# Attention on TensorE: the last four transposes of a unit moved between the two halves of the next scores

## The reference, cut to what matters

```
q, k, v = (x @ Wq + bq), (x @ Wk + bk), (x @ Wv + bv)      # 16 heads of 32
scores = einsum('bhqd,bhkd->bhqk', q / sqrt(32), k) + attention_bias   # (2, 16, 2048, 2048)
scores = where(mask, -inf, scores)
probs = softmax(scores, axis=-1)
ctx = einsum('bhqk,bhkd->bhqd', probs, v)
```

## Time and profile before

| what | value |
|---|---|
| median of 3 runs | 3473.58 us (3472.29 to 3478.68) |
| the profiled execution | 3475.8 us, span 3474.0 us |
| TensorE matmuls busy | 3408.8 us, 98% |
| GpSimd busy | 2395.8 us, 69% |
| VectorE busy | 2343.6 us, 67% |
| ScalarE busy | 2278.9 us, 66% |
| TensorE, transposes of probabilities (L1288) | 8192, 1023.6 us |
| TensorE, scores (L1267) | 2048, 700.7 us |
| TensorE, V products (L1307) | 16384, 500.3 us |

### The profile page before, as it was taken

How to read it: one execution, slowest core, us unless ns; L and a number is a source line. 1 busy time by engine, 2 the same in 40 slices (tenths; PEclk the granted TensorE clock), 3 DMA queues, 4 the chain that set the end, 5 groups by cost and what they waited for, 6 DMA issues and landing times. The chain is left out here.

```text
span 3474.0 us, 84659 instructions
## 1 busy us (share of the span) xinstructions
PE 3408.8 (98%) x33299; PEld 2692.7 (78%) x33299; DVE 2343.6 (67%) x5039; ACT 2278.9 (66%) x3399; POOL 2395.8 (69%) x942
## 2 busy tenths in 40 slices
PE   7999989999999999999999999999999999999998
PEld 3444448888888888888888888888778888887886
DVE  7776758888888888888888888888623232332333
ACT  2433449999999999999999999999622212221321
POOL 1222249999999999999999999999643324232322
PEclk8999999999999999999999999999999999999998
DMA  6666599888898988898888998888644544564463
GB/s 215 225 235 239 197 367 349 325 337 331 333 401 329 338 331 333 341 389 337 332 332 329 367 370 334 331 327 329 246 144 154 167 137 157 164 191 143 154 210 124
DMA packets 342721, 954.80 MB, mean 275 GB/s; under 512 B 33204, under 2 KB 190004, under 8 KB 267576
## 3 DMA queue, kind: packets, MB, share of 16 engines
q1 hardware_dynamic: 337108, 940.95, 73.4%
q10 hardware_dynamic: 5220, 8.42, 0.6%
HBM read 849.63 MB, written 99.62 MB: 273 GB/s over the span
## 5 line engine op out<-in xcount | busy, mean ns | idle before, releaser
L1249 POOL TENSOR_TENSOR at_tiles<-at_tiles,at_negmask 128x1920 f32<-128x1920 f32 x509 | 1950.7, 3896 | 29.9 <-DMA at_tiles<-in_bias 19.0
L1349 ACT ACTIVATE at_tiles<-at_tiles,at_rmin 128x2048 f32<-128x2048 f32 x512 | 1030.5, 2013 | 2.4 <-DVE at_rmin L1409 2.4
L1288 PE MATMUL at_ps_p<-consts,at_tiles 128*128 128x128 f32 x8192 | 1023.6, 272 | 1.7 <-ACT at_prob_t L1359 1.3
L1288 PEld LDWEIGHTS at_ps_p<-consts,at_tiles 128*128 128x128 f32 x8192 | 936.3, 139 | 72.5 <-DVE at_prob_t L1420 2.0
L1359 ACT ACTIVATE at_prob_t<-at_ps_p 128x512 f32<-128x512 f32 x1664 | 898.2, 603 | 125.0 <-PE at_ps_p L1288 124.9
L1409 DVE CUSTOM_DVE_ANT_0 at_tiles<-at_ps_s,at_tiles,at_rmin 128x1024 f32<-128x1024 f32 x512 | 655.0, 1279 | 171.7 <-PE at_ps_s L1273 171.0
L1267 PE MATMUL at_ps_s<-at_k_stack,at_q_stack 128*128 128x512 f32 x2048 | 700.7, 438 | 8.1 <-DVE at_rmin L1409 6.1
L1409 DVE CUSTOM_DVE_ANT_0 at_tiles<-at_ps_s,at_tiles 128x1024 f32<-128x1024 f32 x512 | 623.9, 1219 | 24.5 <-POOL at_tiles L1249 22.2
L1307 PE MATMUL at_ps_c<-at_prob_t,at_v 128*32 128x128 f32 x16384 | 500.3, 274 | 1.0 <-DVE at_ctx_rows L1437 1.0
L1307 PEld LDWEIGHTS at_ps_c<-at_prob_t,at_v 128*32 128x32 f32 x16384 | 431.6, 110 | 44.2 <-issue 43.0
L1267 PEld LDWEIGHTS at_ps_s<-at_k_stack,at_q_stack 128*128 128x128 f32 x2048 | 310.8, 191 | 62.5 <-issue 51.5
(11 more groups left out here) (239 smaller groups left out, 4098.3 us busy)
## 6 DMA issues: line engine op xcount, KB each, us to landing
at_tiles<-in_bias SPq DMA_DIRECT2D x512, 1024.0 KB, 6.3
ff_w_card<-w_mix SPq DMA_DIRECT2D x256, 256.0 KB, 2.7
ff_w_card<-in_W SPq DMA_DIRECT2D x192, 256.0 KB, 2.9
at_k_stack<-k_hi SPq DMA_DIRECT2D x128, 256.0 KB, 5.6
at_k_stack<-k_lo SPq DMA_DIRECT2D x128, 256.0 KB, 5.6
negm<-em_mask_out SPq DMA_DIRECT2D x32, 512.0 KB, 6.5
at_q_stack<-q_hi SPq DMA_DIRECT2D x128, 128.0 KB, 5.3
at_q_stack<-q_lo SPq DMA_DIRECT2D x128, 128.0 KB, 5.3
```

The lines of the kernel that those rows point to most:

```text
L1249: pool.tensor_tensor(tiles[s][:, 0:PCOLS], tiles[s][:, 0:PCOLS], negm[s][:, 0:PCOLS], ALU.add).then_inc(s_pool, 1)
L1288: last = pe.transpose(ps_p[k][:, y * P:(y + 1) * P], tiles[s][:, t * P:(t + 1) * P], ident)
L1349: act.activation(tiles[s][:, :], tiles[s][:, :], ACT.Exp, bias=rmin[:, s, 1:2], scale=-1.0, accum_out=rsum[:, s:s + 1]).then_inc(s_exp, 1)
```

## The change

In TensorE's loop over g, two calls move up by one place: chunk 3 of unit u + 1, and chunk 3 of unit u + 3, each from behind `qk(.., 0)` to ahead of it. No other engine's order changes, and no instruction comes or goes.

```diff
                 pv(pr - 1)
                 qk(u + 4, 1)
+                transposes(u + 1, (3,))
                 qk(u + 5, 0)
-                transposes(u + 1, (3,))
                 transposes(u + 2, (0, 1))
                 qk(u + 5, 1)
...
                 pv(pr)
                 qk(u + 6, 1)
+                transposes(u + 3, (3,))
                 qk(u + 7, 0)
-                transposes(u + 3, (3,))
```

## The result

| | before | changed |
|---|---|---|
| median (7 runs each) | 3475.66 us | 3463.23 us (3458.51 to 3469.22) |
| profiled execution, span | 3475.8, 3474.0 | 3461.7, 3459.9 |
| ratio, 95% interval | | 0.9965 (0.9953 to 0.9977) |

The change makes the kernel 0.35% faster, 12.4 us by the medians; the prediction was 10.7 less, 3462.9. (The median of before is that of seven runs now; the three shown ahead of the prediction had 3473.58.)

What follows compares the result with a forecast made beforehand. TensorE was taken as the bound, GpSimd close behind; -12.7 us from start distances behind the mask plus 2.0 us of bank waits gave -10.7, thus 3462.9 us from the 3473.58 median; range 3456 to 3473, forecast's own 3458 to 3468.

Steps and rivals of the forecast that it cites:

- The joint: TensorE behind the mask matmul, 254 half-groups: transposes there instead of scores swap 0.15 us of start distances for 0.10; 12.7 us less.
- The twin: On TensorE, the context parts' transpose, also 128x128 f32, starts 0.07 us behind a mask matmul; taken as the moved transposes' price.
- The loop through VectorE: Scores overwrite PSUM that VectorE reads; their weight load could come 0.07 us sooner, of which 0.05 would be used, costing nothing.
- The delayed scores: Scores behind the moved transposes end about 0.4 us later, before VectorE takes them up; cost zero.
- the cover: VectorE's 1.28 us operation on its earlier half, hiding the later scores; 0.4 us of it was to stay.
- The moved chunk: Its transposes wait for a PSUM bank VectorE's copy empties: free when steady, 2.0 us lost at the start and mask changes.
- rival 1: Mask-to-transpose on TensorE takes 0.12 us, so the move gains nothing: 3475.6 us, chance 0.08.
- rival 2: GpSimd becomes the bound, its waits for bias tiles inherent: 3.871 us a unit, gain 2 us, 3471.5 us; chance 0.09.
- the cap of 17.8: Most that the room before TensorE's weight load waits for VectorE permits: 254 half-groups times 0.07 us.
- rival 3: VectorE's loop binds sooner or mask-to-transpose is cheaper: gain up to what 0.07 us permits, 3455.8 us; chance 0.07.
- rival 4: Moved transposes wait for their bank in every two-copy half-group, 127 times 0.22 us: slower, 3489 us; chance 0.08 with like delays.

## Why the prediction was right

- *What bounds.* TensorE, with GpSimd close behind. It held: less time on TensorE came out as less time of the kernel, and the steady half-group was the same with half of GpSimd's work.
- *The joint.* Put at 0.05 a half-group, 12.7 us; it is 0.053, 13.5 us. The twin (the transpose of the context parts behind a mask) was the right row: 0.07 foretold, 0.06 to 0.07 found. The wide mask showed what the prediction only argued: the scores need some 0.12 behind the start of a mask, and a longer mask covers it. That it is their weight load stays argued. With the mask between the scores, or widened, the move gains nothing; in the wide case the reordered stretch is neutral to 0.01, and the extra 0.017 lies behind it.
- *The closeness.* 3462.9 was foretold and 3463.2 measured, but that is partly luck. The kernel before has 3475.66 in seven runs, not the 3473.58 that the forecast was taken from. By the difference it was 10.7 foretold against 12.4 measured; attention alone became 11.9 shorter, and some 2 us lie outside it.
- *The rule of the Trainium skill* ("TensorE: Matmul & The Clock Gate", section "LDWEIGHTS (loading the stationary operand)"). By it, loads of equal columns would have cost alike behind the mask, and the gain would have been nothing. The runs side with the rows: a mask of 256 columns is free ahead of the scores and costs 0.05 ahead of a transpose.
- *The loop through VectorE.* Room 0.07, of which 0.05 was to be used. It is used, and no steady wait came. There are three half-groups where VectorE starts late for a reason that the traces don't show, and there the change gains nothing. One such place, before at 657.41 and in the changed kernel at 656.80:

```profile
656.80 1.28 DVE L1409 CUSTOM_DVE_ANT_0 at_tiles<-at_ps_s,at_tiles,at_rmin 128x1024 f32<-128x1024 f32 x1 [1.29 <-PE at_ps_s L1273]
...
658.15 0.30 PEld L1267 LDWEIGHTS at_ps_s<-at_k_stack,at_q_stack 128*128 128x128 f32 x2 [0.30 <-DVE at_rmin L1409]
```

The load waits 0.30 where it waited 0.25, and the half-group takes 8.04 in both kernels: the slack that used to absorb part of the lateness is spent.

- *The delayed scores* cost nothing, as foretold; 0.46 us of the cover stays. Four more transposes ahead are 4 x 0.11 = 0.44 more; with them VectorE waited 0.05 a half-group.
- *The moved chunk.* Put at 2.0 us, measured 1.6 for attention as a whole. It is free in the steady state, and late after changes of masks, as foretold. But the sum fits by luck: its parts were 0.6, 0.5 and 0.9, and what the traces show at these places is -0.2, 1.8 and -0.6, with 0.45 at the first change of masks, for which nothing was set down. After the second change three of four half-groups lost 0.4 to 0.6 each, and one 0.2; an episode is not paid once, as the prediction had it. Nor did the backlog grow by 0.3 each time: after the third change the changed kernel lost nothing, where the kernel before had lost 0.59. Which change of masks is late differs from kernel to kernel, and there is one trace of each. Even the kernel that moves only the chunk of u + 1, for which no such loss was expected, has one of 1.8 us at the third change (four half-groups from 1994.10 to 2026.85, where 30.9 is steady). So how much of the 1.6 is the moved chunk's, and how much is one execution's chance, is not shown. Part of the loss at the second change was the bank's: free it sooner, and 0.46 of 1.77 is left there. What makes the transfers late is open.
- *The rivals.* The joint is not nothing (rival 1). GpSimd's waits shrank, 18.1 to 9.9, as the argument against rival 2 said. The gain did not reach the cap of 17.8 (rival 3), and the moved chunk waits in few groups, not in all (rival 4).

## What to carry to other kernels

When an engine is the bound and has no waits, look at the distances between the starts of unlike instructions: here a short matmul in front of scores left a time uncovered that a longer one covered, most likely the next weight load. So try the neighbour with the shortest load behind the short matmul, or a longer matmul in front of the longest load. Find the price of a new neighbour in its nearest twin elsewhere in the trace. And before counting on it, measure how much room the next loop has; here it was 0.07 us a half-group. Small losses that come and go need more than one trace: a sum that fits can be made of parts that do not.

## What the runs showed of the hardware

- Behind a 128-column bf16 matmul the next one could start 0.07 later if it was an f32 transpose, while f32r scores in effect cost 0.12; behind a 256-column one both cost 0.12.
- The same two f32r score matmuls with the mask behind them took 0.54 from the first start to the mask's in the changed kernel, 0.55 with eight transposes ahead and 0.56 with the wide mask and the move, though the order around them is the same. I did not expect it and have no cause for it.
- Where TensorE had to wait for VectorE, the load started 0.05 after VectorE's end. There a half-group took 8.04 us in both kernels, 0.29 and 0.34 over the steady one, for waits of 0.25 and 0.30.
